# Gated linear attention between two expert layers: the order of one head pair's work on five engines is changed

## The reference, cut to what matters

```python
x = x + 0.5 * ffn(layernorm(x))
x = x + attention(layernorm(x))
x = x + 0.5 * ffn(layernorm(x))

def attention(x):                       # 16 heads, d_k = d_v = 64, T = 4096
    q, k, v = x @ W_q, x @ W_k, x @ W_v
    a = sigmoid(x @ W_gate + b_gate)    # one decay for each token, head and key channel
    for t in range(T):                  # S: 64 x 64 for each head
        S = a[t][:, None] * S + k[t][:, None] * v[t][None, :]
        out[t] = q[t] @ S
    return out @ W_o
```

## Time and profile before

| | before |
|---|---|
| median of 3 runs | 2367.86 us |
| profiled execution, its own time | 2370.87 us |
| span of the profiled execution | 2369.1 us |
| attention on PE, first gate matmul to last W_o matmul | 771.7 to 1570.2 us |
| one supertile, from the same gather to the same gather | 98.97 us |
| PE, DVE, ACT, POOL busy in one supertile | 92.7, 63.9, 55.3, 7.6 us |
| DMA in one supertile | 4% of 16 engines |

### The profile page before, as it was taken

How to read it: one execution, slowest core, us unless ns; L and a number is a source line. 1 busy time by engine, 2 the same in 40 slices (tenths; PEclk the granted TensorE clock), 3 DMA queues, 4 the chain that set the end, 5 groups by cost and what they waited for, 6 DMA issues and landing times.

```text
span 2369.1 us, 38722 instructions
## 1 busy us (share of the span) xinstructions
PE 2026.0 (86%) x14479; PEld 1795.1 (76%) x14480; DVE 1300.2 (55%) x2904; ACT 1185.8 (50%) x1927; POOL 265.9 (11%) x267
## 2 busy tenths in 40 slices
PE   5159999999995999999999999973499999999990
PEld 5148888888985777778877788772398899988880
DVE  6335555555555558575575755645354545565544
ACT  1045556655553646465464654710356556665530
POOL 1720000000002101001010000007300000000227
PEclk9999999999997999999999999975699999999995
DMA  6242212222122000000000000002411221222214
GB/s 260 98 150 81 98 62 80 71 98 80 51 88 71 19 1 19 10 11 19 1 19 10 10 1 1 1 1 97 152 55 69 92 80 49 73 91 98 81 58 142
DMA packets 95409, 150.92 MB, mean 64 GB/s; under 512 B 9583, under 2 KB 76678, under 8 KB 94068
## 3 DMA queue, kind: packets, MB, share of 16 engines
q1 hardware_dynamic: 83008, 116.46, 14.4%
q0 software_dynamic: 12288, 32.91, 4.4%
HBM read 98.84 MB, written 51.15 MB: 63 GB/s over the span
## 4 chain that ended last, share of the span: by engine, by line
PE 66%; DVE 10%; PEld 7%; POOL 6%; issue 5%; ACT 4%; DMA 1%; PEldq 1%; POOLq 0%; DVEq 0%; SPq 0%
PE bank L538 27%; PE bank L557 12%; PE bank L609 8%; PE bank L696 4%; PEld bank L557 4%; POOL expert_in L426 4%; PEld bank L538 3%; PE bank L633 3%; PE bank L679 2%; PE bank L684 2%; POOL halves L433 2%; PE bank L502 2%; DVE wide L1306 1%; DVE wide L1281 1%; PE bank L519 1%
## 5 line engine op out<-in xcount | busy, mean ns | idle before, releaser
L538 PE MATMUL bank<-halves 128*128 128x512 f32 (+2 forms) x3744 | 771.0, 366 | 22.3 <-DVE halves L1116 22.3
L538 PEld LDWEIGHTS bank<-halves 128*128 128x128 f32 x3744 | 649.2, 191 | 128.2 <-issue 24.6
L557 PE MATMUL bank<-halves 128*128 128x256 f32 (+1 forms) x3288 | 403.1, 283 | 3.0 <-issue 3.0
L557 PEld LDWEIGHTS bank<-halves 128*128 128x128 f32 (+1 forms) x3288 | 397.3, 189 | 5.7 <-issue 4.8
L798 ACT ACTIVATE temp<-bank,bias_now 128x512 f32<-128x512 f32 (+1 forms) x312 | 200.2, 642 | 368.5 <-PE bank L538 368.1
L1129 DVE SCALAR_TENSOR_TENSOR temp<-bank,bias_fc,temp 128x512 f32<-128x512 f32 (+1 forms) x312 | 216.0, 692 | 226.8 <-ACT temp L798 223.3
L609 PE MATMUL bank<-halves 128*128 128x512 f32 x1152 | 285.4, 399 | 2.0 <-DVE halves L1256 2.0
L1136 DVE TENSOR_TENSOR halves<-temp,halves 128x512 fp32r<-128x512 f32 (+1 forms) x312 | 197.9, 634 | 126.6 <-ACT halves L754 123.5
L609 PEld LDWEIGHTS bank<-halves 128*128 128x128 f32 x1152 | 211.9, 189 | 49.2 <-DVE halves L1256 2.4
L433 POOL DMA_INDIRECT halves<-expert_out,read_slot x96 | 104.5, 1089 | 1171.2 <-DMA expert_out<-rows 651.2
L754 ACT ACTIVATE halves<-temp 128x512 fp32r<-128x512 f32 (+1 forms) x313 | 184.9, 591 | 9.9
(11 more groups left out here) (158 smaller groups left out, 2227.0 us busy)
## 6 DMA issues: line engine op xcount, KB each, us to landing
expert_out<-rows SPq DMA_DIRECT2D x144, 128.0 KB, 1.7
wide<-in_L_ffn_w_c_fc SPq DMA_DIRECT2D x16, 1024.0 KB, 5.4
wide<-in_L_ffn_w_gate SPq DMA_DIRECT2D x16, 1024.0 KB, 7.4
wide<-in_L_ffn_w_c_proj SPq DMA_DIRECT2D x16, 1024.0 KB, 5.4
wide<-expert_in SPq DMA_DIRECT2D x32, 512.0 KB, 4.9
expert_in<-halves SPq DMA_DIRECT2D x9, 1024.0 KB
x<-in_L_attn_x SPq DMA_DIRECT2D x4, 1024.0 KB, 9.6
out_x<-x SPq DMA_DIRECT2D x32, 128.0 KB, 2.4
```

The lines of the kernel that those rows point to most:

```text
L538: m = pe.matmul(bank[at + b][:, 0:w], a[:, kc, j * P:(j + 1) * P], v[:, kc, 0:w], start=(i == 0), stop=(i == len(ps) - 1))
L557: mm = pe.matmul(bank[4 + t % 2][0:m, 0:C], a[:, j, o:o + m], v[:, j, :], start=(k == 0), stop=(k == len(ps) - 1))
```

## The change

The pair loop is reordered on all engines, and POOL gets four instructions for each pair.

- Gates: `far` becomes two tiles, used in turn. PE makes the gate of g+2 at the head of pair g; ACT does its Exp there (`gate_exp`) and its Ln at the end of pair g (`gate_log`). The gate of pair 1 is Exp'ed and Ln'ed after all eight value copies, and `sum_logs` of pair 1 goes between the second and third `add_output`.
- PE: outputs of g-1 stand ahead of the turned keys and scores of g (`turn_keys` is split off `scores`). `turn_x` stands after the outputs of pair 6, ahead of the keys of pair 7. `values` of the next supertile stands ahead of `out_projection`, with its two banks exchanged, and its second part waits for the split of the last outputs.
- ACT: key copy and output copy stand ahead of `decays`. The first value copy stands ahead of `decays` of pair 0, the other seven behind it.
- DVE: the state scan of g stands right behind the mask of g, ahead of `scaled` of g+1; split of outputs g-1 stands ahead of the mask of g.
- POOL makes `carry` and `factors` (`spread_carry`), and the gathers of later tiles stand between these.

The diff, without the unchanged lines, the new semaphores, a shift of two tiles by 8 columns and the clearing of the second `far`:

```diff
-near, far = (t.rearrange("p (h a n) -> p a h n", h=2, a=SUPER) for t in (near_all, far_all))
+far_all = [far_all, part(temp, 512, 2 * RUN)]
+near, *far = (t.rearrange("p (h a n) -> p a h n", h=2, a=SUPER) for t in (near_all, *far_all))
...
+        def spread_carry(s, g):
+            G = s * NPAIR + g
+            now = carry[:, g % 2, :]
+            pool.wait_ge(near_made, G + 1)
+            nc.gpsimd.tensor_copy(now[:, 1:2], near[:, 0, 0, 0:1]).then_inc(carry_made, 1)
+            nc.gpsimd.tensor_tensor(now[:, 2:SUPER + 1], near[:, 1:SUPER, 0, 0], near[:, 0:SUPER - 1, 1, HALF - 1],
+                                    ALU.mult).then_inc(carry_made, 1)
+            nc.gpsimd.tensor_copy(now[:, SUPER + 1:SUPER + 2],
+                                  near[:, SUPER - 1, 1, HALF - 1:HALF]).then_inc(carry_made, 1)
+            pool.wait_ge(carry_made, 3 * G + 3)
+            wait_past(pool, state_kept, G)
+            nc.gpsimd.tensor_copy(factors.rearrange("p (n c) -> p n c", n=DH),
+                                  now.unsqueeze(1).to_broadcast([P, DH, SUPER + 2])).then_inc(factors_made, 1)
+        def gather_pair(i):
+            if i >= SUPER:
+                pool.wait_ge(combined, i - SUPER + 1)
+            for k in range(TOPK):
+                gather(got4[:, i % SUPER, k, :], k, i, rows_got[i % SUPER])
...
-            for i in range(TILES):
-                if i >= SUPER:
-                    pool.wait_ge(combined, i - SUPER + 1)
-                for k in range(TOPK):
-                    gather(got4[:, i % SUPER, k, :], k, i, rows_got[i % SUPER])
+            for i in range(2 * SUPER):
+                gather_pair(i)
+            pool.wait_ge(att_cleared, ATT_CLEARS)
+            for s in range(NSUP):
+                for g in range(NPAIR):
+                    spread_carry(s, g)
+                    if 0 < g <= SUPER and s + 2 < NSUP:
+                        gather_pair((s + 2) * SUPER + g - 1)
...
         def project_z(s, g):
+            wait_past(pe, z_used, s * NPAIR + g)
...
         def project_qk(s, g):
...
-                    pe.wait_ge(z_used, s * NPAIR + 1)
...
+                    elif n == 1 and s:
+                        pe.wait_ge(ot_split, s * NPAIR)
...
-                        m = pe.matmul(bank[5 + n % 2][:], a[:, kc, b * P:(b + 1) * P],
+                        m = pe.matmul(bank[6 - n % 2][:], a[:, kc, b * P:(b + 1) * P],
...
-        def scores(s, g):
+        def turn_keys(s, g):
...
+        def scores(s, g):
+            G = s * NPAIR + g
...
+            elif s:
+                pe.wait_ge(wo_added, s * SUPER)
...
-            if g:
-                pe.wait_ge(state_kept, G)
+            wait_past(pe, state_kept, G)
...
         def supertile(s, last):
...
-                G = s * NPAIR + g
+                if g + 2 < NPAIR:
+                    project_z(s, g + 2)
+                if g:
+                    outputs(s, g - 1)
+                if g + 1 == NPAIR and not last:
+                    pe.wait_ge(qk_made, s * NPAIR + NPAIR)
+                    turn_x(s + 1)
...
-                elif g + 1 < NPAIR:
-                    pe.wait_ge(z_used, G + 1)
-                    project_z(s, g + 1)
+                turn_keys(s, g)
...
-                if g + 1 == NPAIR and not last:
-                    turn_x(s + 1)
-                if g == 0:
-                    project_qk(s, 1)
-                else:
-                    outputs(s, g - 1)
...
-                if 0 < g < NPAIR - 1:
+                if g + 1 < NPAIR:
...
-            out_projection(s)
...
-                pe.wait_ge(wo_added, s * SUPER + SUPER)
-                pe.wait_ge(state_kept, s * NPAIR + NPAIR)
+            out_projection(s)
...
-        def log_decay(s, g, first=False):
+        def gate_exp(s, g):
...
-            if not first:
-                act.wait_ge(qk_made, G)
-            gate = far[:, :, :, 0:HALF]
+            if G >= 2:
+                act.wait_ge(qk_made, G - 1)
...
-            nc.scalar.activation(gate, z, ACT.Exp, scale=-1.0, bias=bias_gate[:, g:g + 1]).then_inc(z_used, 1)
-            act.wait_ge(z_used, G + 1)
+            nc.scalar.activation(far[g % 2][:, :, :, 0:HALF], z, ACT.Exp, scale=-1.0,
+                                 bias=bias_gate[:, g:g + 1]).then_inc(z_used, 1)
+        def gate_log(s, g):
+            gate = far[g % 2][:, :, :, 0:HALF]
+            act.wait_ge(z_used, s * NPAIR + g + 1)
...
         def decays(s, g):
...
-            nc.scalar.activation(near_all, far_all, ACT.Exp, scale=-1.0).then_inc(near_made, 1)
+            wait_past(act, carry_made, 3 * G)
+            wait_past(act, qk_made, G)
+            nc.scalar.activation(near_all, far_all[g % 2], ACT.Exp, scale=-1.0).then_inc(near_made, 1)
...
-            nc.scalar.activation(far_all, far_all, ACT.Exp).then_inc(far_made, 1)
+            nc.scalar.activation(far_all[g % 2], far_all[g % 2], ACT.Exp).then_inc(far_made, 1)
         def turned_keys(s, g):
...
-        def values(s):
-            for n in range(2 * SUPER):
+        def values(s, part_=range(2 * SUPER)):
+            for n in part_:
...
-                copy(v_sb[:, n // 2, n % 2 * 512:n % 2 * 512 + 512], bank[5 + n % 2][:]).then_inc(v_copied, 1)
-                if n == SUPER:
-                    log_decay(s, 1)
+                copy(v_sb[:, n // 2, n % 2 * 512:n % 2 * 512 + 512], bank[6 - n % 2][:]).then_inc(v_copied, 1)
+            if part_.stop == 2 * SUPER:
+                gate_exp(s, 1)
+                gate_log(s, 1)
         def supertile(s, last):
...
-                if 0 < g < NPAIR - 1:
-                    log_decay(s, g + 1)
...
-                    log_variance(s + 1)
+                    inverse_deviation(s + 1)
+                if g + 2 < NPAIR:
+                    gate_exp(s, g + 2)
+                if g:
+                    split_o(s, g - 1)
+                if g + 1 == NPAIR and not last:
+                    split_x(s + 1)
...
-                elif not last:
-                    split_x(s + 1)
-                if g:
-                    split_o(s, g - 1)
-                if g == SUPER + 1 and not last:
-                    inverse_deviation(s + 1)
+                if g + 2 < NPAIR:
+                    gate_log(s, g + 2)
+                if g == SUPER and not last:
+                    log_variance(s + 1)
...
-                log_decay(s + 1, 0)
+                gate_exp(s + 1, 0)
+                gate_log(s + 1, 0)
...
+                values(s + 1, range(1))
...
-                values(s + 1)
+                values(s + 1, range(1, 2 * SUPER))
...
-        log_decay(0, 0, first=True)
+        gate_exp(0, 0)
+        gate_log(0, 0)
...
         def sum_logs(s, g):
...
-            back, ahead = far_all[:, RUN - 1::-1], far_all[:, RUN:2 * RUN]
+            back, ahead = far_all[g % 2][:, RUN - 1::-1], far_all[g % 2][:, RUN:2 * RUN]
...
-            v.tensor_copy(carry[:, g % 2, 1:2], near[:, 0, 0, 0:1])
-            v.tensor_tensor(carry[:, g % 2, 2:SUPER + 1], near[:, 1:SUPER, 0, 0], near[:, 0:SUPER - 1, 1, HALF - 1],
-                            ALU.mult)
-            v.tensor_copy(carry[:, g % 2, SUPER + 1:SUPER + 2], near[:, SUPER - 1, 1, HALF - 1:HALF])
...
-            for o, i, w, part_, at in ((q, bq, far, lower, first), (q, bq, near, upper, second),
-                                       (kd, bk, near, lower, first), (kd, bk, far, upper, second)):
+            away = far[g % 2]
+            for o, i, w, part_, at in ((q, bq, away, lower, first), (q, bq, near, upper, second),
+                                       (kd, bk, near, lower, first), (kd, bk, away, upper, second)):
...
-            f, kv, st = (t.rearrange(by_value, n=DH) for t in (factors, bank[7][:, 0:DH * (SUPER + 2)], states))
-            dve.wait_ge(qk_made, G + 1)
-            steps.after(v.tensor_copy(f, carry[:, g % 2, :].unsqueeze(1).to_broadcast([P, DH, SUPER + 2])))
+            kv, st = (t.rearrange(by_value, n=DH) for t in (bank[7][:, 0:DH * (SUPER + 2)], states))
+            dve.wait_ge(factors_made, G + 1)
...
         def supertile(s, last):
...
-                if g:
-                    chain(s, g - 1)
-                if g + 1 < NPAIR:
+                if 0 < g < NPAIR - 1:
...
-                elif not last:
+                elif g and not last:
...
+                if g:
+                    split_o(s, g - 1)
...
+                chain(s, g)
...
-                    if g:
-                        split_o(s, g - 1)
...
-            chain(s, NPAIR - 1)
-            split_o(s, NPAIR - 2)
...
+                if b == 1 and not last:
+                    sum_logs(s + 1, 1)
...
+        sum_logs(0, 1)
```

More of the change, by code:

```diff
@@ L72 @@
 CONSTS = 4
-ATT_CLEARS = 6
+ATT_CLEARS = 7
 assert ROWS % CLEAR_ROWS == 0 and NG == 3 and Y_TILES % 2 == 0
@@ L189, in macaron @@
         kdt = part(temp, 0, SUPER, P)
-        state = part(temp, 1024, NPAIR, DH)
-        factors = part(temp, 1536, DH * (SUPER + 2))
+        state = part(temp, 1032, NPAIR, DH)
```

(5 more changed lines are left out.)

## The result

The changed kernel takes 2338.16 us (median of 4 runs, 2337.30 to 2340.45), the kernel before 2369.38 (2366.57 to 2375.08): a ratio of 0.9867, 95% interval 0.9846 to 0.9887. It is 31 us faster; 42 were forecast.

What follows compares the result with a forecast made beforehand. PE, busy 86%, was taken to be held up by the order of hand-overs, 6.3 us idle a supertile. Waits of 60.3 removed less 18.3 paid anew, net 42: 2368 - 42 = 2326 us; range 2312 to 2354.

Steps and rivals of the forecast that it cites:

- the fourth value part: PE's values at the supertile boundary: wait for ACT's second value copy, 1.15 late, seven times, 8.1 us paid anew.
- the start: Supertile 0: pair 2's gate waits 1.5 and the key copy comes late; together 2.9 us paid anew.
- the end: Last supertile: pair 7 still waits for mask and scan, 2.4 us, and W_o for its split, 1.5.
- The outputs of pair 6: PE before pair 7, no gate to hide behind while DVE normalises: 0.15 allowed, 8 times, 1.2 us.
- the additions of pair 7: PE's additions, as ACT copies x before the keys: may wait 0.15, seven times, 1.1 us.
- PE's need of 8.43 us a pair: PE's time for a pair without waits, from the old trace: 8.67 less 0.24 lost to a wait.
- Gates two ahead: Second far tile has Ln ready a pair earlier; DVE's 0.79 us wait for Ln becomes spare.
- the ring: Old order's dependency loop in a pair: gate, Exp, Ln, sum_logs, mask, scaled, scan, outputs; DVE runs 7.9 of 8.7 us.
- the 1.87: Upper end for POOL's long spread instruction: 1.87 us, the longest POOL instruction in the earlier trace.
- GpSimd holding VectorE: Rival: POOL's spread stalls DVE's scans and copies; in part 2348 us, chance 0.13; in full 2388, chance 0.08.
- the 1.56 from which it would decide: DVE standstill per pair from which the full GpSimd rival decides: 0.9 + 42 / 64 = 1.56 us.
- The wait that changes its name: Rival: late scaled delays ACT's key copy, the 6.3 us return at the additions; about 2366; no change, chance 0.09.

Runs made afterwards that it cites:

- e1: Changed kernel with PE's turned keys ahead of outputs, and ACT's key copy ahead of the output work, in pairs 1 to 5; 2335.33 us.
- e5: Changed kernel with keys ahead of outputs in pairs 1 to 5, two value copies ahead of pair 0's decays, and state kept after scaled keys; 2321.15 us.
- e7: Changed kernel with outputs of g-1 behind additions of g in pairs 1 to 4, output copies and splits later, state kept after scaled keys; 2365.50 us.
- e4: Changed kernel with carried decays and factors made by VectorE, as in the kernel before, GpSimd only issuing gathers; 2345.94 us.
- e3: Changed kernel with the gate of g+1, not g+2, made at the head of pair g from pair 1 on, Exp and Ln at once; 2348.70 us.
- e8: Changed kernel with GpSimd spreading the carried decays four times over, one after the other, same result; 2338.61 us.

## Why the prediction was right, and where it was off

**The mechanism was right.** The waits of the earlier trace rows were what the order cost; 52.7 us of them became 12.6. Each named remainder is there: the fourth value part (forecast 8.1, listed idle 6.5), the start (2.9; 2.6), the end (2.4 + 1.5; 2.0 + 1.5). The outputs of pair 6, given 0.15, don't wait; the additions of pair 7, given as much, come 0.2 late (851.92 to 853.22 from scores to additions, 1.30 instead of 1.10).

**The term that was mis-sized is PE's need of 8.43 us a pair.** I took it from the old order as a property of the work. It is one of the order: 8.74 with outputs ahead of keys. 94.90 - 93.5 = 1.4 a supertile, about the 5 x 0.31 of pairs 1 to 5, and ten of the eleven missing us in seven. e1's first pair and e5 show that the order of PE's blocks does it, and with e7 (there through a subtraction) the time goes with the number of changes of weight shape (four: 8.44, five: 8.6, six: 8.74); e4 rules out GpSimd, and the rows of the pair rule out late operands. That the load is open *because* the shape changes is read from PEld's rows; no run changed a shape alone, so this last step is argued and not shown.

**Gates two ahead were given too much.** The prediction let them open the ring and lend the 0.79 that VectorE waited. e3 shows that ordinary pairs lose no time without it, since the later places of outputs and keys on PE leave 0.89 spare; it is worth 10 us, nearly all in pairs 5 and 6.

**GpSimd** is worth 6 to 8 us (e4), where I had booked nothing but slack; most of it in pair 6, where VectorE has the most to do. Two bounds of its cost were read loosely and decided nothing: three POOL rows, not one, read SBUF at 128 columns (0.28 to 0.29 each), and the 1.87 lies ahead of attention's first matmul; behind it no POOL instruction of that kernel takes over 0.96.

**The rivals.** GpSimd holding VectorE: the effect exists, but even with four copies (e8) it adds 0.36 us to the two scans of a pair, far below the 1.56 from which it would decide. In the changed kernel the scans take 0.69 and 0.67 (medians of 64), no longer than before, since the one copy falls on `scaled` (805.39 to 805.90, beside the row of 805.30). The Trainium skill (SBUF — State Buffer, Who interferes with whom) calls the port pair that the two engines share an exclusive lock. The trace of e8 agrees that each holds the other up; whether one stands still entirely it does not settle, as each grew by less than it overlapped the other (the second scan by 0.26, beside the fourth copy from 902.74 to 903.12). The wait that changes its name, at the additions, did not come in the changed kernel, but e7 made it: that order puts the key copy in PE's way.

**The range.** Its lower end, 2312, is not quite what its reason gives: with start and tail (2.9, 2.4 and 1.5) kept and the other 11.5 free it is 2314. Nothing hangs on it.

## What to carry to other kernels

When blocks of matmuls are reordered, count where the weights' shape changes between neighbours and take PE's need from a trace of that order; without any wait a pair took 8.74 us in one order and 8.44 in another. Put a long block whose operands are ready into the hole where a result is waited for: here `values` while the last outputs are split for W_o, and then W_o while pair 0 of the next supertile is made ready. And an engine's slack is that of its fullest pair: gates ahead and the move to GpSimd paid almost only there.

## What was not expected of the hardware

A wait too short for the profile to list still costs: in e1 the scaled keys' lateness shows only as 4.36 instead of 4.24 us between two starts, since the first weight load can't run ahead. GpSimd's 384-column copy, at 0.51 us, was only half again as long as VectorE's 0.35.
